# Spreading the B rows on TensorE straight from fp32 rows, without the split in three bf16 parts, and moving one inflow product per unit from GpSimd to VectorE

## What is computed

```python
dbc = u @ xproj_w.T
dt = jax.nn.softplus(dbc[..., :dt_rank] @ dt_w.T + dt_b)
Bm = dbc[..., dt_rank:dt_rank + d_state]
Cm = dbc[..., dt_rank + d_state:]
A = -jnp.exp(A_log)
dA = jnp.exp(dt[..., None] * A)
dBu = (dt * u)[..., None] * Bm[:, :, None, :]

def step(h, inp):
    dA_t, dBu_t, C_t = inp
    h = dA_t * h + dBu_t
    return (h, jnp.einsum('bdn,bn->bd', h, C_t))
```

## Time and profile before

| what | value |
|---|---|
| the three timed runs | 1485.69, 1486.5, 1488.8 us |
| their median | 1486.5 us |
| the profiled execution, first to last instruction (span) | 1526.0 us |
| time of the profiled execution outside its span | none is given |
| GpSimd, first and last `dt_times_u` (units 1 and 15) | 89.1 and 866.1 us |
| busy share of the span, TensorE / VectorE / ScalarE / GpSimd | 86 / 81 / 63 / 76% |
| weight loads of TensorE | 50% |

### The profile page before, as it was taken

One profiled execution on the slowest core, in us unless ns is written; L12 is line 12 of the kernel. 1 busy time (PEld: TensorE's weight loads), 2 busy tenths in 40 slices (PEclk: granted clock), 3 DMA queues, 4 the chain that ended last, 5 costly groups with the idle time before them and its releaser, 6 DMA issues.

```text
span 1526.0 us, 19904 instructions
## 1 busy us (share of the span) xinstructions
PE 1319.7 (86%) x6159; PEld 760.5 (50%) x6159; DVE 1240.1 (81%) x1990; ACT 968.7 (63%) x1810; POOL 1154.2 (76%) x683
## 2 busy tenths in 40 slices
PE   6799889889988988988988878988998999997595
PEld 2234334334434433433433334558996666666594
DVE  6999999999999999999999996323335888876376
ACT  6887878878778777787787774214554555542144
POOL 2899999999999999999999992611333555583542
PEclk9999999999999999999999989999999999999698
DMA  5323322333343333342333224131216000011223
GB/s 194 116 86 123 133 106 104 133 119 111 122 129 113 123 105 114 122 127 93 122 133 107 99 104 188 52 82 41 80 52 220 2 1 2 2 55 32 79 68 96
DMA packets 62888, 148.38 MB, mean 97 GB/s; under 512 B 9216, under 2 KB 34304, under 8 KB 53072
## 3 DMA queue, kind: packets, MB, share of 16 engines
q1 hardware_dynamic: 58016, 137.30, 26.6%
q0 software_dynamic: 4768, 9.81, 2.0%
HBM read 134.14 MB, written 18.56 MB: 100 GB/s over the span
## 4 chain that ended last, share of the span: by engine, by line
PE 32%; DVE 25%; issue 15%; POOL 12%; ACT 10%; another core or an unknown queue 3%; DMA 2%; SPq 1%; DVEq 0%; POOLq 0%; ACTq 0%
DVE hh L754 15%; POOL hc L895 8%; DVE hh L739 3%; PE py L423 3%; ACT pa L598 3%; PE pr L1806 3%; PE bank L1352 2%; PE bank L1348 2%; PE bank L1362 2%; POOL dtu L874 2%; PE pr L1820 2%; PE pr L2009 2%; ACT uz L492 1%; PE bank L1268 1%
## 5 line engine op out<-in xcount | busy, mean ns | idle before, releaser
L895 POOL TENSOR_TENSOR hc<-hh,cs 128x1024 f32<-128x1024 f32 x256 | 599.3, 2369 | 3.9 <-ACT st L603 2.6
L423 PE MATMUL py<-hc,ident 128*128 128x512 f32 x1024 | 487.5, 605 | 0.1
L754 DVE TENSOR_TENSOR_SCAN hh<-pa,st,hh 128x512 f32<-128x512 f32 x384 | 466.4, 1265 | 0.5 <-ACT pa L598 0.2
L598 ACT ACTIVATE pa<-dt,w 128x512 f32<-128x512 f32 x512 | 343.8, 684 | 184.4 <-DVE hh L754 183.2
L423 PEld LDWEIGHTS py<-hc,ident 128*128 128x128 f32 x1024 | 198.3, 195 | 220.5 <-issue 211.8
L885 POOL TENSOR_TENSOR hh<-dtu,bs 128x1024 f32<-128x1024 f32 x111 | 262.4, 2365 | 2.4 <-DMA bs<-bcrows 2.4
L739 DVE TENSOR_TENSOR hh<-dtu,pb 128x1024 f32<-128x1024 f32 x145 | 174.3, 1202 | 15.1 <-POOL dtu L874 14.1
L754 DVE TENSOR_TENSOR_SCAN hh<-pa,hh 128x512 f32<-128x512 f32 x128 | 147.8, 1205 | 2.0 <-ACT pa L598 1.0
L1478 POOL DMA_INDIRECT ytoken<-ysort,token x39 | 39.6, 1016 | 112.2 <-ACT ysort L1410 111.6
L335 PE MATMUL pq<-xn,w 128*128 128x512 f32 x248 | 118.0, 600 | 4.0 <-ACT xn L613 2.8
L1851 DVE TENSOR_SCALAR rot<-pr,b 128x128 f32<-128x128 f32 x184 | 51.8, 344 | 50.0 <-PE pr L1820 21.8
(11 more groups left out here) (333 smaller groups left out, 2523.6 us busy)
## 6 DMA issues: line engine op xcount, KB each, us to landing
cs<-bcrows SPq DMA_DIRECT2D x64, 1024.0 KB, 4.6
bs<-bcrows SPq DMA_DIRECT2D x112, 256.0 KB, 4.4
xsorted<-in_pads SPq DMA_DIRECT2D x13, 387.0 KB, 5.3
rot<-in_rot SPq DMA_DIRECT2D x4, 1024.0 KB, 5.0
wx<-in_l_w SPq DMA_DIRECT2D x4, 1024.0 KB, 10.0
ysort<-ytoken SPq DMA_DIRECT2D x14, 256.0 KB
wx<-in_l_w SPq DMA_DIRECT2D x1, 3072.0 KB, 11.2
wx<-in_l_w SPq DMA_DIRECT2D x1, 2304.0 KB, 16.2
```

The source lines that it names most:

```text
L423: i = pe.matmul(py[:, h * CH:(h + 1) * CH], ident[:, :], hc[s % HCS][:, h, :], start=False, stop=n == NS - 1)
L598: act.activation(pa[i % SLOTS][:, :], dt[m % 2][:, h, :], ACT.Exp, scale=wd[m % 2][:, W_A + h * NS + n:W_A + h * NS + n + 1]).then_inc(s_s ...
L754: v.tensor_tensor_scan(hh[s % HHS][:, h, :], pa[i % SLOTS][:, :], hh[s % HHS][:, h, :], 0.0 if first else st[:, m % 2, n, h:h + 1], ALU.mu ...
L895: g.tensor_tensor(hc[s % HCS][:, :, :], hh[s % HHS][:, :, :], cs[j % 2][:, s % CG, :].unsqueeze(1).broadcast_to([P, HF, CH]), ALU.mult).th ...
```

## The change

Three edits go together, and a fourth is beside them.

1. The split is gone: `rank_and_high`, `mid_part`, `rest_of_high` and `low_part` go, and `bc` with them. ScalarE makes one copy of all 128 rows of `pq` in fp32 (`keep_rows`, step 3), in one of two buffers `crow`. `sel` becomes a 128x16 fp32 one-hot matrix, and `spread_b` is an fp32 matmul with 128 rows.
2. `BY_G` goes from (1, 3, 5, 7, 9, 13, 15) to (1, 3, 6, 9, 11, 14). VectorE has ten inflows in a unit, in steps 0, 2, 4, 5, 7, 8, 10, 12, 13 and 15, and GpSimd six; its B rows come in groups of three (`BG`).
3. Waits: `dt_project` and the first `spread_b` of a unit wait for `keep_rows` alone; the copy waits for the DMA to DRAM of the unit two before, and no longer for that of the unit just before.
4. The last states of a sequence's last chunk are kept no more (`followed`, `kept_states`).

```diff
-BG = 4
-BY_G = (1, 3, 5, 7, 9, 13, 15)
+BG = 3
+BY_G = (1, 3, 6, 9, 11, 14)
...
-                sel = sb(k, "sel", [P, 2 * NS], BF16)
+                sel = sb(k, "sel", [P, NS])
...
-                bc = [sb(k, f"bc{i}", [P, CH], BF16) for i in range(2)]
...
-                crow = sb(k, "crow", [P, CH])
-                dtr = crow[P - RK:P, :]
+                crow = [sb(k, f"crow{i}", [P, CH]) for i in range(2)]
...
+                def followed(m):
+
+                    return m // 2 % (NCH // B) < NCH // B - 1
+
+                def kept_states(s):
+
+                    return NS * sum(followed(m) for m in range(s // NS)) + (s % NS + 1 if followed(s // NS) else 0)
...
                     def spread_b(s):
                         if s % NS == 0:
-                            pe.wait_ge(s_low, s // NS + 1)
+                            pe.wait_ge(s_crow, s // NS + 1)
                         if made(BY_V, s) >= 2:
                             pe.wait_ge(s_db, made(BY_V, s) - 1)
-                        pe.matmul(pb[:, :], sel[0:96, s % NS:s % NS + 1].broadcast_to([96, P]),
-                                  bc[s // NS % 2][0:96, :], start=True, stop=True).then_inc(s_b, 1)
+                        pe.matmul(pb[:, :], sel[:, s % NS:s % NS + 1].broadcast_to([P, P]),
+                                  crow[s // NS % 2][:, :], start=True, stop=True).then_inc(s_b, 1)
...
-                    def rank_and_high(m):
+                    def keep_rows(m):
                         act.wait_ge(s_xp, m + 1)
-                        i = act.activation(dtr, pq[P - RK:P, :], ACT.Identity)
-                        if m == 0:
-                            i.then_inc(s_rank0, 1)
-                        if m >= 1:
-                            act.wait_ge(s_cout, 16 * m)
-                        act.activation(crow[0:2 * NS, :], pq[0:2 * NS, :], ACT.Identity).then_inc(s_crow, 1)
                         if m >= 2:
+                            act.wait_ge(s_cout, 16 * (m - 1))
                             act.wait_ge(s_b, len(BY_V) * (m - 1))
-                        act.activation(bc[m % 2][0:4 * NS, :], pq[0:4 * NS, :], ACT.Identity).then_inc(s_hi, 1)
-
-                    def mid_part(m):
-                        act.wait_ge(s_rest, m + 1)
-                        act.activation(bc[m % 2][2 * NS:4 * NS, :], pq[2 * NS:4 * NS, :], ACT.Identity).then_inc(s_mid, 1)
+                        act.activation(crow[m % 2][:, :], pq[:, :], ACT.Identity).then_inc(s_crow, 1)
...
                     def keep_state(s):
+                        if not followed(s // NS):
+                            return
...
                         if m < UNITS:
-                            if n == 4:
-                                rest_of_high(m)
-                            if n == 5:
-                                low_part(m)
                             if n in (10, 11):
                                 factor(m, n - 10)
```

More of the change, by code:

```diff
@@ L202, in layer0_mamba @@
             s_w = [sem(f"mamba_w_in{i}") for i in range(2)]
-            s_xturn, s_xt, s_xv, s_rank0 = sem("x_turned"), sem("xt_by_scalar"), sem("xt_by_vector"), sem("first_rank_kept")
+            s_xturn, s_xt, s_xv = sem("x_turned"), sem("xt_by_scalar"), sem("xt_by_vector")
             s_wneg, s_wexp, s_wtap = sem("a_negated"), sem("a_exp"), sem("taps_made")
             s_u, s_z, s_pre = sem("u_projected"), sem("z_projected"), sem("pre_kept")
-            s_uz, s_xp, s_hi = sem("uz_made"), sem("x_projected"), sem("high_kept")
-            s_rest, s_mid, s_low = sem("high_taken_off"), sem("mid_made"), sem("low_made")
+            s_uz, s_xp = sem("uz_made"), sem("x_projected")
             s_din, s_ra = sem("dt_projected"), sem("relu_abs")
@@ L355, in dt_project @@
                     def dt_project(m, h):
-                        if m == 0:
[L357 to L360, removed]
+                        if h == 0:
+                            pe.wait_ge(s_crow, m + 1)
+                        elif m >= 1:
                             pe.wait_ge(s_ra, 2 * m + 1)
-                        pe.matmul((pq if m >= 1 else py[:, h * CH:(h + 1) * CH])[:, :], wd[m % 2][P - RK:P, W_DT + h * P:W_DT + (h + 1) * P], dtr,
+                        pe.matmul((pq if m >= 1 else py[:, h * CH:(h + 1) * CH])[:, :], wd[m % 2][P - RK:P, W_DT + h * P:W_DT + (h + 1) * P], crow[m % 2][P - RK:P, :],
                                   start=True, stop=True).then_inc(s_din, 1)
@@ L441, in mamba_tensor @@
                     turn_x(2, s_nv, 8)
-                    pe.wait_ge(s_low, 1)
+                    pe.wait_ge(s_crow, 1)
                     pe.wait_ge(s_w[1], 48)
@@ L554, in prep @@
                             if n == 3:
-                                rank_and_high(m)
-                            if n == 5:
-                                mid_part(m)
+                                keep_rows(m)
                             if n == 7:
@@ L644, in mamba_scalar @@
                     act.activation(ab[:, 0, 0:1], eps[:, 0:1], ACT.Sigmoid)
-                    rank_and_high(0)
+                    keep_rows(0)
                     first_abs(0)
-                    mid_part(0)
                     first_abs(1)
@@ L693, in mamba_vector @@
                 def mamba_vector():
-                    def rest_of_high(m):
-                        rows = slice(2 * NS, 4 * NS)
-                        v.wait_ge(s_hi, m + 1)
-                        v.tensor_tensor(pq[rows, :], pq[rows, :], bc[m % 2][rows, :], ALU.subtract).then_inc(s_rest, 1)
-                    def low_part(m):
-                        rows = slice(2 * NS, 4 * NS)
-                        v.wait_ge(s_mid, m + 1)
-                        v.tensor_tensor(bc[m % 2][4 * NS:6 * NS, :], pq[rows, :], bc[m % 2][rows, :], ALU.subtract).then_inc(s_low, 1)
                     def factor(m, f):
@@ L737, in inflow @@
                             v.wait_ge(s_hc, s - HHS + 1)
-                            v.wait_ge(s_st, s - HHS + 1)
+                            v.wait_ge(s_st, kept_states(s - HHS))
                         v.tensor_tensor(hh[s % HHS][:, :, :], dtu[m % 2][:, :, :],
@@ L749, in scan @@
                         if n == 0 and not first:
-                            v.wait_ge(s_st, NS * (m - 1))
+                            v.wait_ge(s_st, kept_states(NS * (m - 1) - 1))
                         for h in range(HF):
@@ L833, in mamba_vector @@
                     first_z(0)
-                    rest_of_high(0)
-                    low_part(0)
                     taps(1)
@@ L883, in inflow @@
                             g.wait_ge(s_hc, s - HHS + 1)
-                            g.wait_ge(s_st, s - HHS + 1)
+                            g.wait_ge(s_st, kept_states(s - HHS))
                         g.tensor_tensor(hh[s % HHS][:, :, :], dtu[m % 2][:, :, :],
@@ L925, in mamba_sync @@
                             sy.dma_start(keep[:, :], a["keep"]).then_inc(s_small, 16)
-                            sy.dma_start(sel[0:96, :], a["sel"]).then_inc(s_small, 16)
+                            sy.dma_start(sel[:, :], a["sel"]).then_inc(s_small, 16)
                             sy.dma_start(number[:, :], a["number"]).then_inc(s_small, 16)
@@ L930, in rows_out @@
                         sy.wait_ge(s_crow, m + 1)
-                        sy.dma_start(bcrows[m], crow[0:2 * NS, :]).then_inc(s_cout, 16)
+                        sy.dma_start(bcrows[m], crow[m % 2][0:2 * NS, :]).then_inc(s_cout, 16)
                     def c_in(j):
@@ L2611, in constants @@
     k["centre"] = np.eye(D, dtype=np.float32) - np.float32(1.0 / D)
-    k["sel"] = (np.arange(96)[:, None] % 32 == np.arange(32)).astype(mybir.dt.np(BF16))
+    k["sel"] = (np.arange(P)[:, None] == np.arange(NS)).astype(np.float32)
     k["before"] = np.triu(np.ones((P, P), np.float32), 1).astype(mybir.dt.np(BF16))
```

2 lines of the change are left out of this document (removed).

## The result

The changed kernel takes 1514.55 us (median of 4 runs, 1509.55 to 1517.53) against 1487.65 us for the kernel before (4 runs, 1485.69 to 1489.16): ratio 1.0183, 95% interval 1.016 to 1.0206, so slower by some 27 us. The forecast was 1509.5 us.

A forecast was written before the change was run, and what follows sets the result against it. GpSimd set the pace before; TensorE's loop would after. A unit of 57.3 us, 1.8 more, gives 13 x 1.8 = 23.4, with the ends +23: 1486.5 + 23 = 1509.5 us, range 1486 to 1526.

The forecast's parts named there:

- GpSimd and VectorE: Their work in a unit after the change: GpSimd 53.2 us, VectorE 54.1, or 54.9 with statistics.
- An fp32 spread at 0.86 us: Each spread_b on TensorE takes two records, 0.86 us; ten make 8.6 us, bringing TensorE's work to 53.3 us.
- The loop: TensorE's closed round through the gate: 53.3 us of work plus 2.6 of forced idle time, at least 55.9 us.
- The term of 0.4 us for the inflow of step 4: In TensorE's step 3, the spread for step 5 waits for VectorE's inflow of step 4, 0.4 us on average.
- The waits of VectorE: VectorE's loop: 54.9 us plus waits of 0.4 at the gate, 0.5 and 0.5, 56.3 us.
- 0.4 us at the gate: VectorE's gate is late by 0.4 us in each unit, behind TensorE's spread for step 5 and last sum.
- The spread for step 12: VectorE must have this TensorE spread finished, so it stands about 0.5 us more.
- 0.5 us, at the squares: Behind out_project ScalarE's collect comes later, costing VectorE perhaps 0.5 us for the squares.
- The clock: After the idle time at the gate TensorE runs at 1.2 GHz in 7 of 12 units: 1.7 us each, 1.0 on average.
- The ends: Outside units 1 to 13: start -1.6 us, unit 14 +0.6, the stretch from 866.1 +0.5.
- The rival on the other side: TensorE is no bound; units go by VectorE at 54.1 or 54.9 us, kernel 1472 us; chance 15%.

The follow-up runs named there:

- e8: The changed kernel with its ten and six inflows in other steps, GpSimd having (1, 3, 5, 7, 9, 15): ratio 0.9903 to the kernel before, 54.35 us a unit.
- e10: The changed kernel with every fp32 spread issued twice: ratio 1.0891 to the kernel before, 64.55 us a unit at full clock.
- e6: The changed kernel with the last sum ahead of step 5's spread, and step 7's spread behind the D term and first sum: ratio 0.9965, 55.14 us a unit.
- e9: The changed kernel itself, unedited, measured again in a later set: ratio 1.0169 to the kernel before, 57.28 us a unit.
- e7: As e6, with the spread that must wait also put behind the sum in steps 6, 11 and 14: ratio 0.9978 to the kernel before, 55.20 us a unit.
- e4: The changed kernel with B's rows rounded to bf16 and the spread a single bf16 pass: ratio 0.9923 to the kernel before, 54.96 us a unit.
- e1: The changed kernel with the old table of steps (nine inflows on VectorE, seven on GpSimd): ratio 0.9988 to the kernel before, 55.52 us a unit.
- e3: The changed kernel with step 7's spread issued after the D term and first sum: ratio 1.0041 to the kernel before, 55.89 us a unit.
- e5: The changed kernel with the last sum issued ahead of step 5's spread in TensorE's step 3: ratio 1.0045 to the kernel before, 55.76 us a unit.
- e2: The kernel before, keeping its split and bf16 spread, with BG = 3 and the new BY_G: ratio 1.0105, 56.24 us a unit.

## Why the prediction was right

**GpSimd and VectorE.** 23 operations of 2.31 us were to be 53.2 us; GpSimd is busy for 53.3. VectorE was put at 54.1 and 54.9 us; it shows 54.2 and 55.2, and e8's units take 54.1 and 55.2.

**An fp32 spread at 0.86 us.** Right, 0.86 or 0.96 after a wait. TensorE's work of 53.3 us is the 53.5 of the full-clock unit.

For the spacing of matmuls the Trainium skill (TensorE: Matmul & The Clock Gate, Back-to-back issue gap) gives some 131 ns; e10, with 8.59 us for ten spreads of two records, 0.43 us a record, doesn't agree with it.

**The loop.** 53.3 + 2.6 = 55.9 us at full clock was the bound; the trace has 55.96, and e10 shows it closed. The term of 0.4 us for the inflow of step 4 ahead of it hasn't shown in units without statistics; in the one at full clock with them (56.98 us) TensorE waits 0.49 us for that inflow. There VectorE's 55.2 us of work with 0.57 at the gate and 1.19 at the scan of step 10 make the same 57.0.

**The waits of VectorE.** 0.4 us at the gate was 0.58. The spread for step 12 was to cost 0.5, and it costs nothing. The waits for spreads in the first 13 distances are

```profile
DVE hh L718 <- PE pb L409: 17.5, 20, 1.1
```

two in each of the ten distances with a slow stretch, at the inflows of steps 8 and 10, and none in the three at full clock: they show where the clock fell. For ScalarE I had 0.5 us, at the squares; it was 1.19, at the scan of step 10. Neither size nor place was right for these two; in the changed kernel it doesn't matter, as TensorE's loop is longer, and it is what holds e6.

**The clock.** 1.7 us a time and 1.0 on average were forecast; 1.69 us is measured, and 9 stretches in the 12 units, instead of 7. 57.3 us a unit was to be, 57.43 and 57.28 (e9) are the two measurements. That they lie so close is in part luck: the 0.4 us ahead of the spread for step 5 is missing from most units, and the clock, which fell more often than forecast, makes up for most of it.

**The ends.** This is the term that was mis-sized, -0.5 us in sum in the forecast. The start won 3.2 us (e9: 5.3) instead of 1.6: the first `dt_times_u` comes at 85.8 us, before at 89.1. Units 14 and 15 were to lose 1.1 us. They lost 3.0 (58.48 against 55.47) and 6.8 (69.0 against 62.2 from the last `dt_times_u` to the last gate). With 13 x 1.92 = 25.0 the block is 25.0 - 3.2 + 3.0 + 6.8 = 31.6 us longer in the profiled execution (last gate at 959.8, before 928.3). In e9 unit 14 loses 3.2 and the way to the last gate 3.6 us (65.8), and the block is 24.5 us longer: half of the 6.8 us is of one execution. What happens in unit 14:

```profile
886.14 1.12 PE L409 MATMUL pb<-crow,sel 128*128 128x512 f32 x2 [1.56 <-DVE hh L718]
887.10 1.88 PE L426 MATMUL py<-hc,ident 128*128 128x512 f32 x4
894.02 2.05 PE L409 MATMUL pb<-crow,sel 128*128 128x512 f32 x2 [5.05 <-DVE hh L718]
895.86 3.62 PE L426 MATMUL py<-hc,ident 128*128 128x512 f32 x4
```

Without `u_half` TensorE has time to spare and uses it ahead of spreads that wait for an inflow, 1.56 and 5.05 us; then it runs at 1.2 GHz (3.4 us for the sum from 895.86 to 899.27, instead of 1.72), with the sums that were held up behind the spread still to do. I had credited this unit with its smaller work and had not asked what the idle time does to the clock. But e9 has the same idle time of 5.05 us and a way of 65.8 instead of 69.0 us, and e7, which moves these spreads behind the sums, won only 0.6 us on that way over e6, so this is a description and not a cause that was shown.

**The rival on the other side**, that TensorE is no bound and GpSimd's relief shows, would have given 1472 us. The Trainium skill (Perfetto Trace Analysis, Identifying the Most-Contended Engine) would have TensorE's headroom judged by its weight loads, beside the share of peak arithmetic that it does; the weight loads fill 24.2 of 56.0 us in a unit in which TensorE's loop sets the pace, so here this sign misleads. The rule to relieve the busiest engine first held in e4 and e8: where TensorE is out of the way, relieving GpSimd does bring the time down.

## What to carry to other kernels

When an engine that works in order looks free, add up its loop before giving it more: its own work by start-to-start times, and every idle time that it can't avoid because it waits for something that waits for it. Here 5.7 us of added work in a unit were free with one table of steps (e1); 6.6 us cost 1.7 to 1.8% with another, mostly because a slow stretch of the clock that had been hidden now lay on the path, and with a third the same 6.6 us stood in a kernel that is 1.0% faster (e8). In an in-order queue, keep an instruction that must wait for a fresh result out of the place right ahead of work that is ready or that others wait for, and put one that is ready into the idle time that stays.

## What was not expected

The clock went with the single idle time at the gate, and not with TensorE's work. The idle time of 2.44 us ahead of the spread for step 7 was followed by the 1.2 GHz level in 9 of 12 units; with 1.31 us (e3) or 0.46 to 1.39 us (e6) it was never seen in these units, though TensorE did the same work. In e5 this idle time is 1.58 to 1.76 us in the nine of these units that kept their clock and 2.04 to 2.52 in the three that didn't. It is no rule: in the kernel before, 2.43 us were followed by it in some units and not in others. With the bf16 spreads and the new table (e2), where TensorE waits in more places, it came 15 times in the same units.

The part behind the Mamba block takes 554 us in one profile and 591 to 598 in all others, kernel before included. Laid side by side, the changed kernel's two profiles part in two places, by some 8 us within 90 us after the last gate and by some 30 us at 460 to 475 us after it. Why is open; the change doesn't touch these places.
